# Target attention on one core: both score halves ahead of the context, and the context by group over token residues mod 4

## What is computed

```python
b = target_item.shape[0]                                  # 2048
q = (target_item @ W_q).reshape(b, H, HD)                 # H = 4, HD = 32
k = (history_sequence @ W_k).reshape(b, S, H, HD)         # S = 200
v = (history_sequence @ W_v).reshape(b, S, H, HD)
scores = jnp.einsum('bhd,bshd->bhs', q, k) / SCALE
scores = jnp.where(mask[:, None, :] == 0, NEG, scores)
attn = jax.nn.softmax(scores, axis=-1)
out = jnp.einsum('bhs,bshd->bhd', attn, v).reshape(b, A)
return out @ W_o
```

## Time and profile before

| | |
|---|---|
| median of 3 runs | 766.93 us (765.03 to 769.29) |
| the profiled execution | 765.87 us, its span 764.1 us |
| TensorE: matmul, weight load | 578.2 us (76%), 449.7 us (59%) |
| VectorE | 520.7 us (68%) |
| ScalarE | 280.0 us (37%) |
| GpSimd | 305.7 us (40%) |
| DMA, whole run | 219.18 MB, mean 287 GB/s |
| loads of history | 128 of 832 KB and 128 of 768 KB |
| loads of masks | 64 of 100 KB |

### The profile page before, as it was taken

One profiled execution on the slowest core, in us unless ns is written; L12 is line 12 of the kernel. 1 busy time (PEld: TensorE's weight loads), 2 busy tenths in 40 slices (PEclk: granted clock), 3 DMA queues, 4 the chain that ended last, 5 costly groups with the idle time before them and its releaser, 6 DMA issues.

```text
span 764.1 us, 41709 instructions
## 1 busy us (share of the span) xinstructions
PE 578.2 (76%) x18665; PEld 449.7 (59%) x18665; DVE 520.7 (68%) x577; ACT 280.0 (37%) x909; POOL 305.7 (40%) x1123
## 2 busy tenths in 40 slices
PE   6877777777787777778777777878767777877776
PEld 5655665556566565556556555656656555655655
DVE  4475767776866767876776777686676777677660
ACT  2142334334433433433333433443343443343342
POOL 3624343453443344344344334344434434534420
PEclk9999999999999999999999999999999999999998
DMA  8578688788889788798978879898988979897940
GB/s 339 213 260 296 247 315 297 287 316 303 312 285 334 261 289 324 279 337 293 328 265 316 309 275 313 299 330 289 330 270 286 329 278 334 279 324 266 318 143 6
DMA packets 49808, 219.18 MB, mean 287 GB/s; under 512 B 5888, under 2 KB 16656, under 8 KB 49760
## 3 DMA queue, kind: packets, MB, share of 16 engines
q1 hardware_dynamic: 49056, 217.60, 80.1%
q0 software_dynamic: 704, 1.05, 0.4%
HBM read 217.58 MB, written 1.05 MB: 286 GB/s over the span
## 4 chain that ended last, share of the span: by engine, by line
PE 41%; ACT 17%; DVE 14%; DMA 10%; issue 9%; POOL 7%; SPq 1%; POOLq 0%; DVEq 0%; ACTq 0%
ACT p_pad L391 16%; PE ps_c L287 15%; PE ps_s L256 11%; DMA mask<-r_mask 10%; DVE blocks L456 8%; PE ps_p L270 7%; POOL u_pad L200 6%; PE ps_y L297 4%; DVE probs_t L480 3%; DVE weights L476 2%; PE ps_p L349 2%; POOL bias L204 1%; PE ps_y L304 1%; ACT probs L382 1%; DMA w_in<-L_rec_W_o 1%
## 5 line engine op out<-in xcount | busy, mean ns | idle before, releaser
L456 DVE STREAM_TRANSPOSE blocks<-hist 128x1536 f32<-128x1536 f32 (+1 forms) x256 | 454.4, 1812 | 6.4 <-DMA hist<-r_history_sequence 6.4
L200 POOL COPY u_pad<-u_sb 32x32 f32<-32x32 f32 x1024 | 233.6, 228 | 60.6
L287 PE MATMUL ps_c<-hist,p_pad 64*32 64x128 f32 x12800 | 221.4, 274 | 5.3 <-issue 4.8
L391 ACT ACTIVATE p_pad<-ps_p,own 128x200 f32<-128x200 f32 x512 | 169.7, 442 | 116.1 <-PE ps_p L270 116.1
L204 POOL TENSOR_SCALAR bias<-mask 128x200 f32<-128x200 int32 x64 | 56.4, 881 | 371.5 <-DMA mask<-r_mask 369.8
L256 PE MATMUL ps_s<-blocks,u_pad 128*32 128x200 f32 x4096 | 202.0, 338 | 0.0
L287 PEld LDWEIGHTS ps_c<-hist,p_pad 64*32 64x32 f32 x12800 | 185.3, 106 | 26.7 <-issue 19.4
L465 DVE CUSTOM_DVE_ANT_0 neg_score<-ps_s,bias 128x200 f32<-128x200 f32 x64 | 23.4, 366 | 198.9 <-PE ps_s L256 198.9
L256 PEld LDWEIGHTS ps_s<-blocks,u_pad 128*32 128x32 f32 x4096 | 121.0, 110 | 52.2 <-issue 8.8
L270 PE MATMUL ps_p<-probs_t,place_sel 128*64 128x112 f32 x1024 | 65.2, 271 | 82.8 <-DVE probs_t L480 82.8
L270 PEld LDWEIGHTS ps_p<-probs_t,place_sel 128*64 128x64 f32 x1024 | 51.3, 140 | 100.1 <-DVE probs_t L480 71.6
(11 more groups left out here) (42 smaller groups left out, 122.3 us busy)
## 6 DMA issues: line engine op xcount, KB each, us to landing
hist<-r_history_sequence SPq DMA_DIRECT2D x128, 832.0 KB, 7.9
hist<-r_history_sequence SPq DMA_DIRECT2D x128, 768.0 KB, 6.6
mask<-r_mask SPq DMA_DIRECT2D x64, 100.0 KB, 5.1
x_sb<-r_target_item SPq DMA_DIRECT2D x21, 48.0 KB, 9.0
out<-out_sb POOLq DMA_DIRECT2D x21, 48.0 KB, 4.5
w_in<-L_rec_W_q SPq DMA_DIRECT2D x1, 64.0 KB, 1.8
w_in<-L_rec_W_k SPq DMA_DIRECT2D x1, 64.0 KB, 2.2
w_in<-L_rec_W_v SPq DMA_DIRECT2D x1, 64.0 KB, 5.2
```

What stands on the lines that cost most here:

```text
L200: pool.tensor_copy(to, source[Q * c:Q * c + Q, a]).then_inc(u_pad_ready, 1)
L287: mm = pe.matmul(ps_c[alpha][at:at + Q, 0:D], p_pad[ring][rows, t + par, i, :], hist[2 * ring + i][rows, t + par, :], start=(t == 0), stop ...
L391: op = act.activation(p_pad[p % RING][:, :, :, H * k:H * k + H].rearrange("p t i h -> p (t i) h"), source[:, k // 4], ACT.Copy, scale=own[ ...
L456: dve.transpose(blocks[g % BLOCKS][:, t0:t1].rearrange("p t c k -> p (t c k)"), hist[g % SLOTS][:, t0:t1, :].rearrange("p t d -> p (t d)") ...
```

## The change

- TensorE's `step` does both score halves of the next pair ahead of the wait for the expansion; `transpose_target`, `combine` and `outputs` go between the two halves, one in each ring slot. The two calls of `context` then follow each other.
- `context` takes a group, not a token half, and its four column tiles are token residues mod 4 of this group. Groups 0 and 1 lie side by side in PSUM, so ScalarE copies 256 columns for each `alpha`, and `turn_context` has four matmuls of 32 columns in place of two of 64, with the constant `share_sel`, which VectorE makes.
- SP's history loads wait for the context of their own group; a mask is asked for one pair earlier; the targets one round earlier.
- GpSimd spreads before it makes the bias, and the bias waits for `max_ready`; `u_sb` is double.
- The outputs go to `ps_u`, and are made and stored a step later. The warm-up has 63 transposes.

```diff
-    IDLE_TURNS = 96
+    IDLE_TURNS = 63
-        u_sb = sb("u_sb", [P, H, ROUND])
+        u_sb = [sb(f"u_sb{n}", [P, H, ROUND]) for n in range(2)]
...
-                        wait(sp, ctx_done, 2 * (p - RING) + h + 1)
+                        wait(sp, ctx_done, g - SLOTS + 1)
...
+                    if i == 0 and p == 0:
+                        load_mask(0)
+                    if i == 0 and p + 1 < NP:
+                        load_mask(p + 1)
...
-                if p % RING == 1 and p // RING + 1 < NR:
-                    r = p // RING + 1
-                    wait(sp, x_t_done, r)
+                if (p == 0 or p % RING == 2) and (p + 1) // RING + 1 < NR:
+                    r = (p + 1) // RING + 1
+                    sp.wait_ge(x_t_done, r)
...
+            spread(0)
+            spread(1)
+            pool.wait_ge(u_pad_ready, 32)
             mask_bias(0)
             mask_bias(1)
-            pool.wait_ge(bias_ready, 2)
-            spread(0)
-            spread(1)
             for p in range(NP):
                 if p + 2 < NP:
-                    pool.wait_ge(exp_done, p + 1)
-                    pool.wait_ge(u_pad_ready, 16 * p + 32)
+                    pool.wait_ge(bias_ready, p + 2)
+                    spread(p + 2)
+                    pool.wait_ge(u_pad_ready, 16 * p + 48)
+
+                    pool.wait_ge(max_ready, p + 1)
                     mask_bias(p + 2)
-                    pool.wait_ge(bias_ready, p + 3)
-                    spread(p + 2)
...
-            def context(ring, half):
-                t0, t1 = HALVES[half]
-                for t in range(t0, t1, 2):
+            def context(ring, i):
+
+                for t in range(0, T, 4):
                     for alpha in range(2):
                         rows = slice(64 * alpha, 64 * alpha + 64)
-                        for i in range(2):
-                            for par in range(min(2, t1 - t)):
...
+                        for x in range(min(4, T - t)):
+                            mm = pe.matmul(
+                                ps_c[alpha][Q * x:Q * x + Q, i * D:(i + 1) * D],
+                                p_pad[ring][rows, t + x, i, :],
+                                hist[2 * ring + i][rows, t + x, :],
+                                start=(t == 0), stop=(t + x + 4 >= T),
+                            )
...
             def turn_context():
                 for alpha in range(2):
-                    mm = pe.matmul(ps_y[:, 64 * alpha:64 * alpha + 64], ctx_sb[:, alpha, :],
-                                   par_sel[:, :, :].rearrange("p i r -> p (i r)"), start=True, stop=True)
+                    for i in range(2):
+                        at = 64 * alpha + Q * i
+                        mm = pe.matmul(ps_y[:, at:at + Q], ctx_sb[:, alpha, i, :], share_sel[:, :],
+                                       start=True, stop=True)
...
                 place(q)
                 if ahead:
-                    scores(q + 1, after, 0)
+                    scores(q + 1, (ring + 1) % RING, 0)
+                if targets and (ring == 2 or first):
+                    transpose_target(r + 2 if ring == 2 else 1)
+                if targets and ring == 0 and not first:
+                    combine(r + 1)
+                if ring == 1 and not (isinstance(r, int) and r == 0):
+                    outputs(q - 1)
+                if ahead:
+                    scores(q + 1, (ring + 1) % RING, 1)
                 pe.wait_ge(expanded, q + 1)
                 if not first:
                     pe.wait_ge(ctx_copied, 2 * q)
                     turn_context()
                 context(ring, 0)
-                if ring == 0 and combines:
-                    transpose_target(r + 1)
-                if ring == 0 and not first:
-                    outputs(q)
-                if ahead:
-                    scores(q + 1, after, 1)
-                if ring == 0 and combines:
-                    combine(r + 1)
                 context(ring, 1)
+                if first:
+                    combine(1)
...
-                wait(act, u_pad_ready, 16 * RING * r)
+                wait(act, u_pad_ready, 16 * RING * (r - 1))
...
-                    act.copy(ctx_sb[:, alpha, :], ps_c[alpha][:, 0:D]).then_inc(ctx_copied, 1)
+                    act.copy(ctx_sb[:, alpha, :, :], ps_c[alpha][:, 0:2 * D].rearrange("p (i d) -> p i d", i=2)).then_inc(ctx_copied, 1)
```

More of the change, by code:

```diff
@@ L144, in _, with load_mask @@
             sp.dma_start(x_sb[:, :], target[0:ROUND, :]).then_inc(x_loaded, 16)
+            def load_mask(p):
+                wait(sp, bias_ready, p - RING + 1)
+                rows = mask[p * Q:(p + 1) * Q, :]
+                sp.dma_start(mask_sb[p % RING][:, :],
+                             rows.unsqueeze(1).broadcast_to([Q, H, S])).then_inc(mask_loaded[p % RING], 16)
             for p in range(NP):
@@ L223, in _ @@
                     pool.dma_start(out[r * ROUND:(r + 1) * ROUND, :], out_sb[:, :]).then_inc(out_stored, 16)
-            for r in range((NP - 1) // RING - 1, NR):
+            for r in range(NR - 2, NR):
                 pool.wait_ge(y_copied, r + 1)
@@ L303, in outputs, with step @@
                 for h in range(H):
-                    mm = pe.matmul(ps_y[0:ROUND, P:P + D], ctx_t[:, h, :], w_vo[:, h, :],
+                    mm = pe.matmul(ps_u[0:ROUND, H * ROUND:H * ROUND + D], ctx_t[:, h, :], w_vo[:, h, :],
                                    start=(h == 0), stop=(h == H - 1))
                 mm.then_inc(y_done, 1)
-            def step(q, ring, r, first=False, ahead=True, combines=True):
-                after = (ring + 1) % RING
+            def step(q, ring, r, first=False, ahead=True, targets=True):
                 place(q)
                 if ahead:
-                    scores(q + 1, after, 0)
+                    scores(q + 1, (ring + 1) % RING, 0)
[7 more added lines that the diff above has]
+                    scores(q + 1, (ring + 1) % RING, 1)
                 pe.wait_ge(expanded, q + 1)
@@ L352, in _ @@
             step(0, 0, 0, first=True)
+            step(1, 1, 0)
             with pe.Fori(0, LOOPS) as r:
-                step(3 * r + 1, 1, r)
                 step(3 * r + 2, 2, r)
                 step(3 * r + 3, 0, r + 1)
-            step(NP - 3, 1, NR - 2)
-            step(NP - 2, 2, NR - 2)
-            step(NP - 1, 0, NR - 1, ahead=False, combines=False)
+                step(3 * r + 4, 1, r + 1)
+            step(NP - 2, 2, NR - 2, targets=False)
+            step(NP - 1, 0, NR - 1, ahead=False, targets=False)
+            outputs(NP - 1)
             pe.wait_ge(ctx_copied, 2 * NP)
@@ L375, in copy_combined @@
                 act.wait_ge(u_done, r + 1)
-                wait(act, u_pad_ready, 16 * RING * r)
-                act.copy(u_sb[:, :, :], ps_u[:, 0:H * ROUND].rearrange("p (h n) -> p h n", h=H)).then_inc(u_copied, 1)
+                wait(act, u_pad_ready, 16 * RING * (r - 1))
+                act.copy(u_sb[r % 2][:, :, :], ps_u[:, 0:H * ROUND].rearrange("p (h n) -> p h n", h=H)).then_inc(u_copied, 1)
             def exponent(p):
@@ L413, in store @@
                 wait(act, out_stored, 16 * r)
-                act.copy(out_sb[:, :], ps_y[0:ROUND, P:P + D]).then_inc(y_copied, 1)
+                act.copy(out_sb[:, :], ps_u[0:ROUND, H * ROUND:H * ROUND + D]).then_inc(y_copied, 1)
             copy_target(0)
@@ L449, in _ @@
                               AX.XY, ALU.add).then_inc(own_ready, 1)
+            dve.tensor_reduce(share_sel[:, :], ident[:, :].rearrange("p (x r) -> p r x", x=4),
+                              AX.X, ALU.add).then_inc(own_ready, 1)
             def turn(p, i, half):
```

42 lines of the change are left out of this document (15 added, 27 removed).

## The result

The changed kernel takes 628.99 us (627.65 to 630.32, 4 runs) against 766.72 (765.03 to 769.29, 4 runs): a ratio of 0.820, 95% interval 0.817 to 0.823. 628 was predicted. The profiled execution has 630.32 with a span of 628.5.

The account below looks back on a forecast made before the run. The order of work, one serial chain, bounded the kernel; afterwards the longest loop, TensorE, would. Start 24.6 + 63 x 9.2 + 1.5 + end 20.9 = 626.6, plus 1.8 around it: 628 us, eight-in-ten range 598 to 685.

Parts of the forecast that it names:

- (a): TensorE's own loop in the steady pair: slot 2 8.4, slot 0 9.4, slot 1 9.35, mean 9.05 us.
- The 0.15 for handovers: Added to the longest loop for handovers and uneven landings, giving 9.2 us a pair.
- the 1.5 of the second exponent: First step: `combine(1)` and its copy stand ahead of the second exponent, costing 1.5 us once.
- Masks, `spread`, `u_sb`: GpSimd's earlier mask, `spread` and double `u_sb`: a gain of 0.65 us a pair, no new cost.
- (c): Ring of loads, from a freed slot through landing, turns and scores to context: 17.1 us over two pairs, 8.6 each.
- Rival 1: DMA engines are the bound, with a ceiling of 355 GB/s: 9.6 us a pair, 653 in all; chance 0.14.
- rival 2: Load landings stay at their median, 6.7 not 4.2: 9.8 us a pair, 666 in all; chance 0.12.
- Rival 3: Look-ahead lost: slower than before if first landings exceed 9.9 us; at 11, 804 in all; chance 0.05.
- Rival 4: Scores move, maxima still late, only mask and `u_sb` waits go: 10.5 us a pair, 710; chance 0.05.
- Start: Before the first pair: fewer warm-up turns put the first maximum at 24.6 us, against 28.65.
- End: From the last maximum to the end: 20.9 us, against 18.4 before the change.
- Warm-up: 63 warm-up turns in place of 96 ahead of the loop: 8.8 us in place of 13.43.

Follow-up runs that it names:

- the run meant to show it: The changed kernel with the loop's first turn written out ahead of TensorE's loop: 972.13 us, ratio 1.271.
- holding one link for 1.6: The changed kernel with the loads of group 0 held until both groups' contexts are done: 656.92 us, ratio 0.857.
- the halves: The changed kernel with the context by token halves of both groups, as before the change, and 71 warm-up transposes: 642.76 us, ratio 0.844.
- the order alone: The changed kernel with the mask loads, GpSimd's order and single `u_sb` of before: 715.93 us, ratio 0.937.
- the slowest kernel: The changed kernel with the context by token halves, as before the change, and 63 warm-up transposes: 976.7 us, ratio 1.266.
- the fastest kernel: The changed kernel with token halves, loads and turns ordered by half, fillers in TensorE's waits and 50 warm-up transposes: 614.19 us, ratio 0.806.

## Why the prediction was right, and where it was not

**The steady pair, (a): right.** The mean of the three slots was forecast as 9.05. In the rows above, a slot 0 pair from `place` on is 0.92 + 1.49 + 1.06 + 1.49 + 1.01 + 3.22 = 9.19, where 9.4 was forecast, and the slot 2 pair ahead of it, 305.16 to 313.52, is 8.36, where 8.4 was. The last 54 periods are 8.96 in the mean. `turn_context` cost 1.01 where 1.1 was taken. TensorE is the bound, and `place` follows the context at once.

**The 0.15 for handovers: wrong, and by luck the right size.** The whole mean is (604.97 - 24.53) / 63 = 9.21, against 9.2. But the steady pairs need no such addition. The first nine periods took 96.9 in place of 9 x 8.96 = 80.6: 16.3 more, for which the sum had only the 1.5 of the second exponent. TensorE stood idle for 14.0 of these 97. It waited 3.17, 2.04 and 1.37 for probabilities, 6.6 in all, and about as long without a releaser, mostly in the middle of a context, as in this timeline of the profile after:

```profile
57.72 2.19 PE L290 MATMUL ps_c<-hist,p_pad 64*32 64x128 f32 x128 [0.17 <-issue]
61.73 0.88 PE L290 MATMUL ps_c<-hist,p_pad 64*32 64x128 f32 x39 [1.83 <-issue]
```

Between 57.72 + 2.19 and 61.73 it stood still for 1.83, and queue 8 has a packet at 59.2. Of its 17 packets 12 start between 20 and 90, in the pairs that are slow. That they cause the loss is argued from this; the run meant to show it was lost to the code's position.

**That the total is off by 1 us is luck in part.** The steady rate makes 63 pairs 15 shorter than 63 x 9.2 (63 x 0.24); the first nine periods give back 16.3 - 1.5 = 14.8, and the end 2.6. The rate was right within 3%, and two terms that the sum lacked cancelled what it had too much.

**Masks, `spread`, `u_sb`: the size was wrong.** "Gain: the 11.38 - 10.73 = 0.65 a pair" was 0.23 by the run with these alone. With the new order they are worth 87 us (137.7 - 50.7). Both halves of the reading were off: the 0.65 of the earlier trace rows held `outputs` and the transpose too, and the price of the masks under the new order was never asked.

**The ring of loads, (c): right in size.** 8.6 a pair beside 9.05 was little slack; holding one link for 1.6 cost 28 us as foretold, and the halves, three of whose four loads start later, came out 13 slower. VectorE waited 37.7 for history in all, under the 60 that was to tell rivals 1 and 2.

**Rivals.** Rival 1 fell: 384 and then 388 GB/s, both above its 355. How far the DMA engines are from a bound of their own stays open, with a share of 0.98 beside the 384. For rival 2 the median landing did stay at 6.9, and the loop held nonetheless; why is argued in the prediction, and no run shows it. Rival 3 is real only as a distance: 1.6 of its 5.7 cost 4%. Rival 4 fell too, since the maxima did come earlier. Its 10.5 a pair and 710 are near the 10.56 and 716 of the order alone by coincidence: it had the mask waits gone and the order without effect, and in that run the order is there and the late mask holds it back.

**Start: right.** First maximum at 24.53 against 24.6. VectorE waited 3.0 for the second exponent, where 1.5 was allowed.

**End: 2.6 too small.** From the last maximum 628.5 - 604.97 = 23.5, against 20.9. The timeline of the profile after:

```profile
604.97 0.37 DVE L476 CUSTOM_DVE_ANT_0 neg_score<-ps_s,bias 128x200 f32<-128x200 f32 x1 [1.68 <-PE ps_s L261]
...
614.25 1.91 PE L302 MATMUL ps_y<-share_sel,ctx_sb 128*128 128x32 f32 x8 [2.76 <-ACT p_pad L398]
...
616.10 5.56 PE L290 MATMUL ps_c<-hist,p_pad 64*32 64x128 f32 x200
```

TensorE had waited 2.76 for the expansion, its granted clock from 614.2 to 621.6 was 0.56, and the last `turn_context` and context took 1.91 and 5.56 in place of 1.08 and 3.29. A stall of 1.08 without a releaser stands in the context of pair 62 before that. The tail before the change had a slow context too; I read only its total.

**Warm-up: the term that failed.** "63 warm-up turns in place of 96: 13.43 x 63 / 96" priced the edit by its length alone, as 4.6 gained. It is worth 129. The forecast came out right here because the change carries a number that suits its own code, and nothing in the profile of before says that another would not do.

## What to carry to other kernels

Look at the packets of the instruction queue beside TensorE's count of instructions: when the same kernel with a few more instructions ahead of its loop is tens of per cent slower, with stalls that no engine releases and more packets on that queue, suspect the code's position, as here, and compare edits ahead of the loop at equal position. Break a serial chain by writing down all loops that run beside it, and price each edit under the new order: parts measured alone gave 15.6 and 50.7 of 137.7. The groups, which free two of a pair's four loads early, beat the halves by 13 us here, although the halves take 0.6 a pair less on TensorE (3.10 + 0.66 against 3.29 + 1.08).

## What the runs showed that was not expected

- 33 transposes, 66 instructions, ahead of a loop change the time by 129 us, and 8 transposes, 16 instructions, decide between 187 and 16 packets of code.
- Behind a stall of 6.49 with code arriving in it the granted clock was 0.5, 1.2 GHz: the mean granted clock was 0.844 in the slowest kernel and 0.986 in the changed one.
- 388 GB/s from 130 to 230, with a share of 0.99, in the fastest kernel; the kernel before moved 302 with a share of 0.85, and 418 only while its queue was full.
